# The first two tiles' grouped convolution as six products straight from the loaded rows, and the third tile's rows loaded earlier

## The reference, cut to what matters

```python
out = lax.conv_general_dilated(x, weight, window_strides=(STRIDE,), padding=[(PAD, PAD)],
                               dimension_numbers=('NCH', 'OIH', 'NCH'), feature_group_count=GROUPS)
...
result = jnp.einsum('bsi,oi->bso', x, W) + b
...
return result + combined
```

## Time and profile before

| | |
|---|---|
| median of three runs | 549.06 us (548.24 to 549.08) |
| the profiled execution, its own time | 548.2 us |
| its span in the trace | 546.4 us |
| PE busy | 524.1 us, 96% of the span |
| DVE busy | 312.3 us, 57% |
| POOL busy | 254.9 us, 47% |
| ACT busy | 121.3 us, 22% |
| granted PE clock, mean | 0.997 of full speed |

### The profile page before, as it was taken

The page is one execution under the profiler, slowest core; times in us unless marked ns, Lnnn a source line. Parts: engine busy times, 40 slices in busy tenths (PEclk is TensorE's granted clock), DMA queues, the critical chain, the costliest instruction groups (busy, mean ns, idle before and its releaser), DMA issues.

```text
span 546.4 us, 14325 instructions
## 1 busy us (share of the span) xinstructions
PE 524.1 (96%) x5717; PEld 446.5 (82%) x5717; DVE 312.3 (57%) x488; ACT 121.3 (22%) x289; POOL 254.9 (47%) x121
## 2 busy tenths in 40 slices
PE   5897999999999889899999999999999999999997
PEld 4675877887887778788988989889889898898896
DVE  4479998797776796345253374463543633634411
ACT  5633433434434231011011011010110110101100
POOL 0038767757747295661552642633615516336100
PEclk9999999999999899999999999999999999999999
DMA  8794455555578326514414244143142241341111
GB/s 314 245 382 171 161 202 189 190 187 207 196 220 239 102 90 186 158 43 121 122 47 151 96 62 150 54 112 126 62 130 101 57 156 70 91 136 62 40 40 38
DMA packets 57209, 75.21 MB, mean 138 GB/s; under 512 B 6432, under 2 KB 43488, under 8 KB 57184
## 3 DMA queue, kind: packets, MB, share of 16 engines
q1 hardware_dynamic: 56960, 74.48, 42.9%
q10 hardware_dynamic: 224, 0.36, 0.3%
HBM read 58.03 MB, written 16.79 MB: 137 GB/s over the span
## 4 chain that ended last, share of the span: by engine, by line
PE 86%; issue 4%; DVE 4%; POOL 3%; ACT 1%; DMA 0%; SPq 0%; DVEq 0%; POOLq 0%; ACTq 0%
PE bank L595 49%; PE bank L502 19%; PE bank L576 6%; PE bank L634 4%; PE bank L436 4%; PE bank L449 2%; PE bank L478 1%; POOL work L1100 1%; DVE parts L923 1%; POOL work L1093 1%; DVE mixes L988 1%; ACT parts L736 1%; DVE y_t L916 0%; DMA cst<-in_consts 0%; DVE y_t L894 0%
## 5 line engine op out<-in xcount | busy, mean ns | idle before, releaser
L595 PE MATMUL bank<-early,parts 128*128 128x320 f32 (+1 forms) x1152 | 207.2, 337 | 4.2 <-POOL mixes L1156 2.3
L595 PEld LDWEIGHTS bank<-early,parts 128*128 128x128 f32 x1152 | 184.6, 188 | 21.4 <-POOL mixes L1156 2.6
L502 PE MATMUL bank<-late,parts 128*128 128x512 f32 x512 | 129.8, 404 | 5.2 <-ACT parts L736 3.4
L502 PEld LDWEIGHTS bank<-late,parts 128*128 128x128 f32 x512 | 93.6, 191 | 26.6 <-ACT parts L736 4.0
L1152 POOL TENSOR_TENSOR xs<-raw 128x1024 f32<-128x1024 f32 x14 | 27.1, 1937 | 156.7 <-DMA raw_turned<-x_scratch 156.7
L595 PE MATMUL bank<-late,parts 128*128 128x512 f32 x384 | 94.1, 394 | 0.0
L923 DVE TENSOR_TENSOR parts<-y_t,parts 128x512 fp32r<-128x512 f32 x64 | 90.4, 1433 | 2.0 <-ACT parts L736 0.6
L595 PEld LDWEIGHTS bank<-late,parts 128*128 128x128 f32 x384 | 70.9, 188 | 16.0
L1100 POOL TENSOR_TENSOR work<-work 128x512 f32<-128x512 f32 x32 | 46.2, 1446 | 49.3 <-DVE work L931 48.2
L1051 DVE TENSOR_TENSOR qk<-bank,qk 128x256 f32<-128x256 f32 x16 | 6.8, 424 | 103.1 <-ACT qk L821 103.1
L736 ACT ACTIVATE parts<-y_t 128x512 fp32r<-128x512 f32 x64 | 39.5, 630 | 91.0 <-DVE y_t L980 49.4
(11 more groups left out here) (107 smaller groups left out, 472.7 us busy)
## 6 DMA issues: line engine op xcount, KB each, us to landing
xs<-in_x SPq DMA_DIRECT2D x16, 512.0 KB, 3.3
work<-in_x SPq DMA_DIRECT2D x16, 512.0 KB, 3.2
x_scratch<-work SPq DMA_DIRECT2D x16, 512.0 KB, 3.0
raw<-x_scratch SPq DMA_DIRECT2D x128, 64.0 KB, 2.8
raw_turned<-x_scratch SPq DMA_DIRECT2D x128, 64.0 KB, 2.5
work<-x_scratch SPq DMA_DIRECT2D x16, 512.0 KB, 3.6
out_tokens<-work SPq DMA_DIRECT2D x15, 512.0 KB, 2.7
stage<-in_wearly SPq DMA_DIRECT2D x8, 576.0 KB, 3.9
```

Source lines behind the costliest of these rows:

```text
L502: last = mm(bank[4 + h][:, :], parts[:, p, a, c, :], signs[:, c, h * HALF:(h + 1) * HALF], start=(k % 16 == 0), stop=(k % 16 == 15))
L595: return mm(dst, parts[:, p, a, c, :], w(b, c), start=(k == 0), stop=(close and k == 23))
```

## The change

For tiles (0, 0) and (0, 1) the convolution is made with six products per block, straight from `raw`: no sums or differences are formed, and `raw_turned` isn't loaded. In the code the six are four instructions per `n` and `g`, two of 128 columns and two of 64; a tile is still 64 instructions of PE, with 6144 columns where there were 4096. `band` now holds the plain taps; the combined ones go to a new tile `taps`, made by DVE from a further input `tapin`, which is loaded into the unused half of `raw_turned`. DVE makes two additions per half of the result instead of five in all. The halves are by token columns, and each waits only for its own products. From tile (1, 0) on the convolution is as before, under the name `product_filter`. SP issues the 16 loads of the third tile's rows ahead of `bias1` and of the last two stores of `x1`, and POOL forms that tile's inputs ahead of the first two residuals' bias. The diff, cut to its core:

```diff
+        taps = sb("taps", [P, 2, GROUPS, S])
...
+        tap_src = raw_turned[:, 1, :, :].rearrange("p n q -> p (n q)")
+        tap_block = [tap_src[:, j * GROUPS * S:(j + 1) * GROUPS * S].rearrange("p (g n) -> p g n", g=GROUPS) for j in range(4)]
...
-            sp.dma_start(band[:, :, :, :].rearrange("p a g n -> p (a g n)"), toep).then_inc(band_loaded, 16)
+            sp.dma_start(band[:, :, :].rearrange("p a n -> p (a n)"), toep).then_inc(band_loaded, 16)
+            sp.dma_start(tap_src, tapin).then_inc(taps_loaded, 16)
...
             sp.wait_ge(pads_zeroed, 2)
-            load_raw(0, 0, False)
+            load_raw(0, 0)
             replace_x1(late_i, 0)
             next_chunk(late_i)
-            load_raw(0, 0, True)
             replace_x1(late_i, 1)
...
             sp.dma_start(xs[:, 0, :], late_pairs[3]).then_inc(late_loaded[3], 16)
-            load_raw(0, 1, False)
...
-            load_raw(0, 1, True)
+            load_raw(0, 1)
             replace_x1(last - 1, 1)
+            sp.wait_ge(z_biased, 2)
+            load_raw(1, 0)
+            load_raw(1, 0, True)
             sp.wait_ge(xb_ready, 2 * TILES)
             sp.dma_start(bias_bc[:, :], bias1.broadcast_to([P, H])).then_inc(bias1_loaded, 16)
             store_x1(last, 0)
...
+            def replace_out(i, p, first=False):
+                both = 4 * i + 2 * p + 2
+                sp.wait_ge(z_biased, both)
+                if not first:
+                    load_raw(i + 1, p)
+                    load_raw(i + 1, p, True)
+                load_row(ctx_row, i + 1, p, ctx_loaded)
+                store_out(i, p, both)
+                sp.wait_ge(out_stored[p], 16 * (i + 1))
+                load_resid(i + 1, p)
+            replace_out(0, 0, True)
+            replace_out(0, 1)
+            with sp.Fori(1, PAIRS - 1) as i:
                 for p in range(2):
-                    both = 4 * i + 2 * p + 2
-                    sp.wait_ge(z_biased, both)
-                    load_raw(i + 1, p, False)
-                    load_raw(i + 1, p, True)
-                    load_row(ctx_row, i + 1, p, ctx_loaded)
-                    store_out(i, p, both)
-                    sp.wait_ge(out_stored[p], 16 * (i + 1))
-                    load_resid(i + 1, p)
+                    replace_out(i, p)
...
-                pe.wait_ge(conv_in_ready, 6 * i + 3 * p + 3)
-            def product_conv(other):
+                pe.wait_ge(raw_loaded[p], (i + 1) * (16 * L8))
+            def product_conv(p, other):
+                low, high = slice(0, S), slice(S, P)
+                steps = ((low, 1, slice(0, P)), (high, 0, slice(0, P)), (low, 0, low), (high, 1, high))
+                for n in range(NBG):
+                    for k, (rows, s, cols) in enumerate(steps):
+                        into = (bank[n // 4], bank[other + n // 4])[k % 2]
+                        at = (n % 4) * P
+                        for g in range(2):
+                            last = mm(into[g * S:(g + 1) * S, at + cols.start:at + cols.stop],
+                                      raw[rows, p, n, s + g * S:s + (g + 1) * S],
+                                      band[rows, s * GROUPS + n % 4, cols], start=(k < 2), stop=(k >= 2))
+                        if n % 4 == 3 and k >= 2:
+                            last.then_inc(conv_done, 1)
+            def inputs_of_filter(i, p):
+                pe.wait_ge(conv_in_ready, 6 * i + 3 * p - 3)
+            def product_filter(other):
...
-                                          src[rows, n, g * S:(g + 1) * S], band[rows, a, n % 4, :], start=True, stop=True)
+                                          src[rows, n, g * S:(g + 1) * S], taps[rows, a, n % 4, :], start=True, stop=True)
...
             for k in range(32):
                 if k == CONV0_AT:
                     pe.wait_ge(y_biased, 2 * TILES)
-                    pe.wait_ge(band_made, 5)
+                    pe.wait_ge(band_loaded, 16)
+                    pe.wait_ge(pads_zeroed, 2)
                     pe.wait_ge(u_ready, 2 * TILES)
                     inputs_of_conv(0, 0)
-                    product_conv(2)
+                    product_conv(0, 2)
                 ffn0_step(last_i, 1, k)
...
                         if h == 1 and k == 12 and ni is not None:
-                            inputs_of_conv(ni, q)
                             if late_ready:
+                                inputs_of_conv(ni, q)
                                 pe.wait_ge(out_scale_ready, 2 * TILES)
                             else:
+                                inputs_of_filter(ni, q)
                                 pe.wait_ge(out_ready, 4 * i + 2 * p)
                         last = z_step(bank[2 + h][:, 0:NH], lambda b, c: early[:, b, c, h * NH:(h + 1) * NH], p, k)
                     last.then_inc(qk_done, 1)
                 if ni is not None:
-                    product_conv(4 + 2 * q)
+                    if late_ready:
+                        product_conv(q, 4 + 2 * q)
+                    else:
+                        product_filter(4 + 2 * q)
...
+            pe.wait_ge(taps_made, 5)
             period1(0, 0, 0, 1, True)
...
-            round_parts(0, 0, z_t, z_biased, z_hi, by_block)
+            round_parts(0, 0, z_t, z_biased, z_hi, by_token)
...
-                if conv:
-                    dve.wait_ge(raw_loaded[0], 32 * L8)
-                    dve.wait_ge(pads_zeroed, 2)
-                    dve.wait_ge(y_done, 2 * TILES)
-                    conv_inputs(0)
...
+            v.tensor_copy(taps[:, 0], tap_block[0]).then_inc(taps_made, 1)
+            v.tensor_tensor(taps[:, 1], tap_block[1], tap_block[3], ALU.add).then_inc(taps_made, 1)
+            dve.wait_ge(taps_made, 2)
+            v.tensor_tensor(taps[low, 1], taps[low, 1], tap_block[2][low], ALU.add).then_inc(taps_made, 1)
+            v.tensor_tensor(taps[high, 1], taps[high, 1], tap_block[2][high], ALU.subtract).then_inc(taps_made, 1)
+            dve.wait_ge(taps_made, 4)
+            v.tensor_scalar(taps[:, 1], taps[:, 1], 0.5, None, ALU.mult).then_inc(taps_made, 1)
...
+            def add_context(i, p, other, halves=(0, 1)):
+                dve.wait_ge(ctx_loaded[p], 16 * (i + 1))
+                dve.wait_ge(z_lo, 4 * i + 2 * p)
+                by_group = lambda made: made[:, :].rearrange("p (n l c) -> p n l c", n=4, l=L8)
+                for h in halves:
+                    zt = z_t[:, :, 64 * h:64 * h + 64].rearrange("p l (n c) -> p n l c", c=CG)
+                    add = row_bc[:, p:p + 1, 64 * h:64 * h + 64].rearrange("p l (n c) -> p n l c", c=CG)
+                    dve.wait_ge(conv_done, 8 * i + 4 * p + 2 * h + 1)
+                    v.tensor_tensor(zt, by_group(bank[h]), add.broadcast_to([P, 4, L8, CG]),
+                                    ALU.add).then_inc(conv_halved, 1)
+                    dve.wait_ge(conv_done, 8 * i + 4 * p + 2 * h + 2)
+                    dve.wait_ge(conv_halved, 4 * i + 2 * p + h + 1)
+                    v.tensor_tensor(zt, by_group(bank[other + h]), zt, ALU.add).then_inc(z_biased, 1)
...
             add_context(0, 0, 2)
-            take_rest(0, 0, z_t, z_hi, z_lo, by_block)
+            take_rest(0, 0, z_t, z_hi, z_lo, by_token)
             scale_out(last, 1, 0)
-            dve.wait_ge(raw_loaded[1], 32 * L8)
-            conv_inputs(1)
             scale_out(last, 1, 1)
...
+                if first:
+                    add_context(ni, q, 4 + 2 * q, (0,))
+                elif ni is not None:
+                    add_filter(ni, q, 4 + 2 * q)
                 dve.wait_ge(wh_hi, t1)
                 v.tensor_tensor(wh_t[:, 1, :], bank[3][:, NH:NH + P], wh_t[:, 0, :].bitcast(F32),
                                 ALU.subtract).then_inc(wh_lo, 1)
-                if ni is not None:
-                    take_rest(ni, q, z_t, z_hi, z_lo, by_block, (0,))
-                    take_rest(ni, q, z_t, z_hi, z_lo, by_block, (1,))
+                if ni is not None and not first:
+                    take_rest(ni, q, z_t, z_hi, z_lo, by_block)
+                elif first:
+                    take_rest(ni, q, z_t, z_hi, z_lo, by_token, (0,))
+                    add_context(ni, q, 4 + 2 * q, (1,))
+                    take_rest(ni, q, z_t, z_hi, z_lo, by_token, (1,))
...
+            def filter_inputs(i, p, first=False):
+                if not first:
+                    pool.wait_ge(conv_done, 4 * i + 2 * p + 4)
+                pool.wait_ge(raw_loaded[p], i * (32 * L8) + 16 * L8)
+                low, high, done = slice(0, S), slice(S, P), 6 * i + 3 * p - 6
...
+            filter_inputs(1, 0, True)
+            add_bias1(0, 0)
+            add_bias1(0, 1)
+            filter_inputs(1, 1)
+            with pool.Fori(1, PAIRS - 1) as i:
                 for p in range(2):
                     add_bias1(i, p)
-                    conv_inputs(i + 1, p)
+                    filter_inputs(i + 1, p)
```

(39 more changed lines are left out.)

55 lines of the change are left out of this document (23 added, 32 removed).

## The result

The changed kernel takes 541.58 us (median of four runs, 540.95 to 542.75) beside 549.07 us for the kernel before (548.24 to 552.66); the ratio is 0.9854, 95% interval 0.9807 to 0.990. It is faster. The profiled execution has a span of 539.6 us and 541.41 us of its own time, 6.8 us under that of before (546.4 and 548.2). The sum gave 6.34.

The account below looks back on a forecast made before the run. PE, busy 96% of the span, was taken as the bound. Terms -1.95 - 0.25 - 0.77 - 1.86 + 0.78 - 2.29 = -6.34 took the profiled 548.2 to 541.9 us; median forecast 542.3, range 540.2 to 545.4.

Parts of the forecast that it names:

- First gap: PE's wait for ACT's rounding before stage 0's last tile closes, -1.95 us; the four products behind it speed up, -0.25.
- Six products for tile (0, 0): Tile (0, 0)'s convolution takes 2.80 us at full clock instead of 3.57 at half clock: -0.77 us.
- Second gap: PE's wait at 200.33 for tile (0, 1)'s convolution inputs closes, as DVE no longer forms them: -1.86 us.
- +0.78: Tile (0, 1)'s convolution, taken as 2.02 us at full clock, costs 2.80 with six products.
- Next in line: Waits PE meets next, `late` weights and `z` of tile (0, 1): no wait, each ready 1.5 us before PE asks.
- Third gap: PE's wait at 224.65 for the third tile's inputs closes through earlier loads and POOL forming them earlier: -2.29 us.
- Restart: Slower products behind a stall, counted only for the four before stage 0's end: 1.20 us against 0.95, -0.25.
- Stage 0: DVE's five tap operations near the start become five others of the same sizes: 0, with 0.5 us either way.

Follow-up runs that it names:

- all-wide version: Changed kernel with all products of the first two tiles' convolutions 128 columns wide, 8192 columns a tile instead of 6144; 542.56 us in one run.

## Why the prediction was right

The range held, and the sum was within half a us of the profiled difference. The median came out at 541.58 and not 542.3: the 0.9 us by which I had set it above the profiled execution weren't there (541.41 and 541.58). By its own steps:

- *First gap, -1.95 and -0.25.* It closed. Scaling ended at 177.9 (forecast 177.8), and PE went through 18 products in 4.31 us. When the gap was put back, by 2.02 us, so was the low clock.
- *Six products for tile (0, 0), -0.77.* Forecast 2.80 us from the two clock levels of the same work; measured 2.84. That is 22 ns a record, or 44 ns a product of two records; the 15.8 ns of the prediction are a record's too, and 31.6 a product's. The all-wide version confirmed that the time goes with the columns.
- *Second gap, -1.86, and +0.78.* Closed; the convolution cost 0.82 more. No run puts this gap back by itself, so its share rests on the traces before and after.
- *Next in line.* The `late` weights were asked for at 205.9, as forecast, and were ready at 202.0. `z` of tile (0, 1) was ready at 211.04 + 0.72 = 211.8 (forecast 211.4), PE went on to tile (0, 1) at 212.7: 1.0 us in hand, not 1.5.
- *Third gap, -2.29.* It closed, but the step credited it to the earlier loads. Undoing them brought back only 0.65 us. What I had missed is that SP and POOL are themselves at the end of the chain that the first two gaps had held up. The number 2.29 came right in the sum because the gap closed either way; as an account of what the edit of the loads is worth in the changed kernel it was wrong (0.9 us). As an addition to the kernel before, the same edit does close the gap, at a ratio of 0.993.
- *Restart.* This is the term that was mis-sized. I counted 0.25 us of slower restart behind the first gap and forgot it behind the other two. Timeline rows with and without the stall give it: 5.44 + 1.86 + 2.03 = 9.33 before for 48 products, 7.20 after, 2.13 saved for 1.86 of stall; likewise 2.56 for 2.29 at tile (0, 1). With 0.27 twice, the sum is -6.9, the profile's difference 6.8.
- *What the sum is set against.* It starts from one execution of the kernel before, a quick one. In the later sets of 7 to 19 runs the medians of that kernel are 550.6 to 551.5 us, beside 541.7 and 542.1 for the change in two of them: 8.5 to 8.9 us, more than the sum or the profiled difference. Where the slower executions of the kernel before lose their time isn't shown, since none of them was traced.
- *Stage 0.* The five other operations on the taps took as long as the old ones, and PE's wait behind them was 1.65 us instead of 1.73.

## What to carry to other kernels

Follow a stall to all that hangs on it before pricing the stalls behind it: here the third one went almost by itself, because the engines that caused it had been late for the same reason as the first. Price a gap in a busy PE by its idle time, plus the slower restart, plus what a lower clock costs when it comes: here 1.5 us in some executions and nothing in others. More columns in the same instructions can be cheaper than forming fewer columns' inputs on a busy engine: 0.8 us a tile here, against gaps of 2.

## What the hardware showed that I had not expected

- The clock is not a fixed cost of a stall, and the length of the stall alone doesn't decide it. After stalls of 1.95, 1.95 and 2.02 us before the last tile of stage 0 it fell to 0.50 each time. Before tile (0, 0)'s 37th product it stayed at 1.00 after stalls of 1.67 and 1.86 us, and fell in another execution after 1.90, where the 12 products took 3.48 us instead of 2.03. The wait of 1.65 to 1.74 us behind the operations on the taps stands in ten of the profiled executions, and 0.50 followed in two of them. It followed a wait of 1.55 us in one execution of the changed kernel (at 44.60; the next 8 products took 3.02 us instead of 2.1), and it didn't follow the longest, 2.29 us before tile (0, 1)'s 37th product. After 0.69 us it stayed.
- Where PE's record has more such places the time scatters more: the kernel before ranged from 545.7 to 553.2 us in 17 of 19 runs (the other two took 554.4 and 555.9), the change with the loads undone, beside it, from 542.6 to 544.1. The clock doesn't make all of this scatter: ten of the 19 had the same mean clock of 0.994 and spans from 545.6 to 551.4 us. A start with 3.1 us of lost issue was seen too.
- DVE and POOL hold each other up in the order in which they start. Of two operations that overlapped, the second was longer by about what was left of the first: by 2.1 to 2.5 us where DVE came second, by 1.0 where POOL did. POOL started 0.37 us ahead in one execution and DVE 0.04 us ahead in another, and with that a stall of 1.95 us was there or wasn't.
